# One of two shifted copies on VectorE, and tile 7's projection moved ahead of its scores, in a transformer block on one core

## What is computed

```python
h = _layernorm(x, ln1_g, ln1_b)
x = _attention(h, h, sa_wq, sa_wk, sa_wv, sa_wo, sa_bo) + x
h = _layernorm(x, ln2_g, ln2_b)
x = _attention(h, cond_emb, ca_wq, ca_wk, ca_wv, ca_wo, ca_bo) + x
h = _layernorm(x, ln3_g, ln3_b)
p = h @ ff_w1 + ff_b1
a, gate = (p[..., :D_FF], p[..., D_FF:])
h = a * jax.nn.gelu(gate, approximate=False) @ ff_w2 + ff_b2
return h + x
```

## Time and profile before

| | us |
|---|---|
| median of 3 runs | 1036.98 |
| lowest and highest | 1036.61, 1037.45 |
| profiled execution, its own time | 1036.71 |
| its span, first to last instruction | 1034.9 |
| TensorE matmul busy | 977.6 |
| VectorE busy | 822.6 |
| ScalarE busy | 621.2 |
| GpSimd busy | 401.2 |

### The profile page before, as it was taken

The page is one execution under the profiler, slowest core; times in us unless marked ns, Lnnn a source line. Parts: engine busy times, 40 slices in busy tenths (PEclk is TensorE's granted clock), DMA queues, the critical chain, the costliest instruction groups (busy, mean ns, idle before and its releaser), DMA issues.

```text
span 1034.9 us, 29709 instructions
## 1 busy us (share of the span) xinstructions
PE 977.6 (94%) x12770; PEld 739.3 (71%) x12770; DVE 822.6 (79%) x940; ACT 621.2 (60%) x1152; POOL 401.2 (39%) x380
## 2 busy tenths in 40 slices
PE   8999999999999999999999999997999999999998
PEld 6666666666666777666666666665678888888887
DVE  4788888889999877989888889998868898554433
ACT  4756656676766766676666676665754544443322
POOL 5114543444553344545534344431333345701000
PEclk9999999999999999999999999998999999999999
DMA  8695545475363644474564654564310001100000
GB/s 183 181 200 126 120 84 129 98 138 126 72 134 71 146 108 99 100 148 96 93 142 98 122 122 82 124 178 80 71 39 22 1 11 43 50 1 21 22 10 31
DMA packets 178114, 96.27 MB, mean 93 GB/s; under 512 B 141120, under 2 KB 158016, under 8 KB 177600
## 3 DMA queue, kind: packets, MB, share of 16 engines
q1 hardware_dynamic: 177984, 94.38, 41.3%
HBM read 56.60 MB, written 12.58 MB: 67 GB/s over the span
## 4 chain that ended last, share of the span: by engine, by line
PE 47%; issue 25%; POOL 16%; DVE 8%; ACT 3%; DMA 0%; POOLq 0%; DVEq 0%; SPq 0%; ACTq 0%
PE W L671 10%; PE SC L749 8%; PE SC L642 7%; POOL X L499 7%; PE W L608 4%; PE W L759 4%; POOL QKT L452 3%; PE W L927 3%; PE W L618 3%; DVE nmax L1249 3%; PE SC L737 2%; POOL QKT L449 2%; PE W L684 1%; ACT OTF L1028 1%; POOL X L487 1%
## 5 line engine op out<-in xcount | busy, mean ns | idle before, releaser
L1013 ACT ACTIVATE PR<-SC,nmax 128x1024 f32<-128x1024 f32 x256 | 286.8, 1124 | 193.9 <-DVE nmax L1249 193.6
L1249 DVE TENSOR_REDUCE nmax<-SC 128x1 f32<-128x1024 f32 x256 | 306.1, 1210 | 58.1 <-PE SC L642 55.8
L1254 DVE STREAM_TRANSPOSE PR<-PR 128x1024 f32<-128x1024 f32 x256 | 314.9, 1236 | 14.4 <-ACT PR L1013 4.4
L499 POOL TENSOR_TENSOR X<-f_raw,X 128x512 f32<-128x512 f32 x128 | 162.8, 1290 | 395.9 <-ACT f_raw L1040 395.9
L671 PE MATMUL W<-PR,V 32*64 32x256 f32 x8192 | 242.0, 380 | 4.1 <-ACT QKF L987 2.5
L642 PE MATMUL SC<-QKT 64*128 64x512 f32 x768 | 232.2, 420 | 8.7 <-ACT PR L1013 8.6
L642 PE MATMUL SC<-QKS 64*128 64x512 f32 x768 | 231.9, 419 | 7.8 <-ACT PR L1013 7.7
L671 PEld LDWEIGHTS W<-PR,V 32*64 32x64 f32 x8192 | 187.4, 132 | 53.5 <-issue 22.3
L642 PEld LDWEIGHTS SC<-QKT 64*128 64x128 f32 x768 | 127.1, 185 | 50.3 <-ACT PR L1013 21.1
L642 PEld LDWEIGHTS SC<-QKS 64*128 64x128 f32 x768 | 127.0, 185 | 49.5 <-ACT PR L1013 21.1
L1040 ACT ACTIVATE f_raw<-W,rden 128x256 f32<-128x256 f32 x256 | 102.1, 485 | 0.7 <-POOL X L499 0.3
(11 more groups left out here) (137 smaller groups left out, 1613.9 us busy)
## 6 DMA issues: line engine op xcount, KB each, us to landing
V<-scratch_v SPq DMA_DIRECT2D x128, 256.0 KB, 4.9
QKS<-QKT SPq DMA_DIRECT2D x96, 256.0 KB, 3.9
scratch_v<-VST SPq DMA_DIRECT2D x32, 256.0 KB, 4.5
wo<-in_L_xattn_sa_wo_dram SPq DMA_DIRECT2D x64, 64.0 KB, 3.8
f_raw<-in_L_xattn_ff_w_dram SPq DMA_DIRECT2D x12, 256.0 KB, 3.0
X<-in_x_dram SPq DMA_DIRECT2D x4, 512.0 KB, 5.3
w_raw<-in_L_xattn_sa_wk_dram SPq DMA_DIRECT2D x16, 128.0 KB, 4.6
w_raw<-in_L_xattn_sa_wq_dram SPq DMA_DIRECT2D x16, 128.0 KB, 3.7
```

What stands on the lines that cost most here:

```text
L499: nc.gpsimd.tensor_tensor(xs, f_raw[:, k % 2, :], xs, ALU.add).then_inc(p_x, 1)
L1013: nc.scalar.activation(PR[:, NT * s + t, :], SC[t % 2][:, :], ACT.Exp, bias=nmax[:, t % 4:t % 4 + 1], accum_out=den[:, s, t:t + 1]).then_i ...
L1249: V.tensor_reduce(nmax[:, t % 4:t % 4 + 1], SC[t % 2][:, :], AX, ALU.max, negate=True).then_inc(d_max, 1)
L1254: V.transpose(tile, tile).then_inc(d_tr, 1)
```

## The change

`gather` makes only the first of the two copies. `add_halves` on VectorE makes the other one first, signals a new semaphore `d_oc`, waits for it and for ScalarE's copy, and adds. VectorE's transpositions of tiles 4 and 5 both follow the maximum of tile 6. ScalarE scales bank 0 ahead of the exponential of tile 5, banks 1 and 2 ahead of that of tile 7, and the last one ahead of that of the next head's tile 0. On TensorE the q/k projection of tile 7 stands directly behind `project_sums`, ahead of the scores of tile 7, and waits for the first scaled bank there. All this holds for iterations that follow a head that is not plain; the last head, outside the loop, gets only the new copy.

```diff
@@ early(h)
+        def early(h):
+            return h > 0 and h - 1 not in PLAIN
@@ TensorE
-                    if h > 0 and h - 1 not in PLAIN and t == 6:
+                    if early(h) and t == 6:
                         project_sums(h - 1)
+                        for g, n, bank in PROJ_AT.get((h, 7), []):
+                            pe.wait_ge(a_op, 4 * (h - 1) + 1)
+                            project(g, n, W[:, bank, :])
...
-                    for g, n, bank in PROJ_AT.get((h, t), []):
+                    for g, n, bank in [] if t == 7 and early(h) else PROJ_AT.get((h, t), []):
...
-                        elif h > 0 and h - 1 not in PLAIN:
-                            pe.wait_ge(a_op, 4 * (h - 1) + 1)
@@ ScalarE
-                    for to, of, col in ((DH, 0, 0), (0, DH, 2 * P)):
-                        nc.scalar.copy(OTF[to:to + DH, BANK:2 * BANK].rearrange("p (a n) -> p a n", a=4),
-                                       W[of:of + DH, :, col:col + P]).then_inc(a_ot, 1)
+                    nc.scalar.copy(OTF[DH:P, BANK:2 * BANK].rearrange("p (a n) -> p a n", a=4), W[0:DH, :, 0:P]).then_inc(a_ot, 1)
...
-                    elif t == 6 and h > 0:
+                    elif t == 5 and early(h):
                         scale_out(h - 1, 0)
+                    elif t == 7 and early(h):
                         scale_out(h - 1, 1)
+                        scale_out(h - 1, 2)
...
                     elif t == 0 and h > 1:
-                        scale_out(h - 2, 2)
                         scale_out(h - 2, 3)
@@ VectorE
-                dve.wait_ge(a_ot, h + 1 + summed(h))
+                dve.wait_ge(s_pv, 8 * (h + 1))
                 dve.wait_ge(s_op, 4 * h)
+                V.tensor_copy(OTF[0:DH, BANK:2 * BANK].rearrange("p (a n) -> p a n", a=4), W[DH:P, :, 2 * P:3 * P]).then_inc(d_oc, 1)
+                dve.wait_ge(d_oc, summed(h))
+                dve.wait_ge(a_ot, h + 1)
                 V.tensor_tensor(OTF[:, 0:BANK].rearrange("p (t a i) -> p a t i", a=4, i=Q),
...
-                    if t > 0 and not (t == 3 and h > 0 or t == 5 and summing):
+                    if t > 0 and not (t == 3 and h > 0 or t in (5, 6) and summing):
                         turn(*divmod(NT * h + t - 1, NT))
                     if t == LAST_BURST and summing:
-                        turn(h, t)
                         add_halves(h - 1)
+                    if t == 6 and summing:
+                        turn(h, 4)
+                        turn(h, 5)
```

More of the change, by code:

```diff
@@ L160, in build_block @@
         s_sc = sem("s_sc"); d_max = sem("d_max"); a_exp = sem("a_exp"); d_tr = sem("d_tr"); d_rd = sem("d_rd")
-        s_pv = sem("s_pv"); a_ot = sem("a_ot"); d_ot = sem("d_ot"); s_op = sem("s_op"); a_op = sem("a_op")
+        s_pv = sem("s_pv"); a_ot = sem("a_ot"); d_oc = sem("d_oc"); d_ot = sem("d_ot"); s_op = sem("s_op"); a_op = sem("a_op")
         s_wt = sem("s_wt"); a_wt = sem("a_wt"); s_m = sem("s_m"); a_m = sem("a_m"); d_m = sem("d_m")
@@ L679, in project_out @@
                 if k == 0:
-                    pe.wait_ge(a_ot, h + 1 + summed(h))
+                    pe.wait_ge(a_ot, h + 1)
                     pe.wait_ge(m_wo[h % 2], 32 * (h // 2 + 1))
```

## The result

| | before | after |
|---|---|---|
| median of 20 runs each, us | 1037.03 | 1032.65 |
| lowest to highest | 1032.94 to 1040.22 | 1030.32 to 1036.67 |
| ratio, 95% interval | | 0.9962 (0.9950 to 0.9974) |
| profiled execution, its own time | 1036.71 | 1032.92 |
| its span | 1034.9 | 1031.1 |

The change gains 4.4 us, 0.4%. Each kernel has one profiled execution, and its own time lies up to 3.4 us off the median of that kernel.

The account below looks back on a forecast made before the run. TensorE, busy 94%, is the engine to fill, but V's eviction would hold the burst: 18 regular iterations x 0.09 = +1.6 us, the others +2.7, in all +4.3 on 1036.71, so 1041.0 us; forecast's own range 1037 to 1045, overall 1034 to 1045.5.

Parts of the forecast that it names:

- The mechanism: Regular iterations: addition 0.53 us earlier, tile 7's scores 0.95 later, then the burst waits for V's eviction and starts 0.09 later.
- The copy: VectorE's copy of one half after the gather, put at 0.66 us, bounds 0.59 to 0.75; addition 0.53 us earlier.
- G: Start of the gather's copies, from which the next burst is counted: G + 12.80 us before the change.
- The largest term: VectorE's maximum of tile 7 behind the start of its scores on TensorE, put at 1.15 us.
- The second: Length of tile 7's projection on TensorE, between output projection and tile 7's scores, put at 1.66 us.
- Two handoffs: ScalarE's scaling to TensorE's projection, put at 0.13 us, and V's eviction to the burst, put at 0.25 us.
- three terms: Bounds: copy 0.59 to 0.75 us, handoff to TensorE 0.06 for 0.13, handoff to the burst 0.20 for 0.25.
- (A): Rival: V's eviction does not hold the burst, TensorE's work does; burst 0.47 us earlier, 1031 us; chance 0.12.
- (B): Rival: VectorE's copy streams two elements at a time and takes 0.40 us; 1035 us in all; chance 0.12.
- (C): Rival: the two copies do not overlap, both reading the same four banks; addition 0.59 us later, 1055 us; chance 0.06.
- My sign of being wrong: Iterations of 21.6 us or less, where 22.1 was forecast; most likely at the step from exponential 0 to the burst.
- The irregular iterations: 9 and 26 together +1.0 us, 11 the whole 0.67, 27 +0.6, 28 and 29 0.2 each; together +2.7.

Follow-up runs that it names:

- early eviction: Kernel after, with ScalarE's eviction of tile 7's q or k projection taken from tile 1 to tile 0, ahead of exponential 0: 1025.87 us, 0.9892 of before.
- late transposition: Kernel after, with VectorE's transposition 6 behind the maximum of the next head's tile 0: 1023.14 us, 0.9878 of before; with 12 more starting matmuls 1022.56 us.
- the order alone: Kernel after, with both copies on ScalarE, the addition waiting for both, and VectorE's order of before: 1044.33 us, 1.0085 of before.
- the copy twice: Kernel after, with VectorE's copy made twice, one behind the other, 25 times: 1051.38 us, 1.0149 of before.
- the copy alone: Kernel before, with only the VectorE copy and its order of transpositions: 1035.82 us, 0.9998; the same with 12 more starting matmuls: 1035.15 us, 0.9985.

## Why the prediction was wrong

**The mechanism stood.** The copy runs beside ScalarE's, the projection fills the time up to tile 7, and the burst then waits for the V eviction. What failed is the size of small terms in the chain of fifteen from G to the burst, and the sign of their sum hung on them. The step that failed most is the one from tile 7's projection to maximum 7: the projection put at 1.66 us, measured 1.57, and the maximum put 1.15 behind its scores, measured 1.03.

| step, after | put at, us | measured | error |
|---|---|---|---|
| copy, then addition, then output projection | 1.43 | 1.47 | +0.04 |
| to the first scaling | 1.21 | 1.21 | 0.00 |
| scaling to tile 7's projection | 0.98 | 0.89 | -0.09 |
| the projection itself | 1.66 | 1.57 | -0.09 |
| first scores of tile 7 to maximum 7 | 1.15 | 1.03 | -0.12 |
| maximum 7, transposition 6, maximum 0, exponential 0 | 3.50 | 3.52 | +0.02 |
| exponential 0 to the V eviction | 2.12 | 2.06 | -0.06 |
| V eviction to the burst | 0.84 | 0.74 | -0.10 |
| G to the burst | 12.89 | 12.49 | -0.40 |

(Scaling 523.49 to projection 524.38 is 0.89, projection to scores 525.95 is 1.57, scores to maximum 526.98 is 1.03, and so on from the rows above.) 18 x 0.40 = 7.2 us would turn the forecast of 1041.0 into about 1034.

**The largest term was a misreading.** I took 527.10 to 528.25 of the earlier trace rows as the time that a maximum needs behind its scores. The last of these rows, which stands between those that I read, says otherwise, and the first two, of the same timelines, have the value that I needed:

```profile
517.18 0.49 PE L642 MATMUL SC<-QKS 64*128 64x512 f32 x1
...
518.21 2.36 DVE L1249 TENSOR_REDUCE nmax<-SC 128x1 f32<-128x1024 f32 x2 [0.79 <-PE SC L642]
...
527.08 1.25 DVE L1254 STREAM_TRANSPOSE PR<-PR 128x1024 f32<-128x1024 f32 x1
```

The last is VectorE's transposition 5 in the kernel before, and it ran until 528.33. The maximum stood behind it in the queue and not behind the scores. An interval between two engines is a latency only if nothing else held the second; here 1.15 was an upper bound and I used it as a value. At 518.21 VectorE did wait for the scores that had started at 517.18: 1.03, as in after.

**The second was of the same kind.** 528.00 to 529.66 was read as the length of a projection. ScalarE's exponential 6, for which the next scores wait, ended at 528.38 + 1.14 = 529.52, and its row sum and handoff come on top. In after, where the exponential is long done, the projection takes 1.57. In before, the next projection, which nothing holds, takes 1.60 (530.55 to 532.15).

**Two handoffs came from far rows.** 0.13 from scaling to TensorE was taken from the last head; here it is 0.05 (523.49 + 0.84 = 524.33, projection at 524.38). I had 0.06 as the other end and priced it rightly at -1.5 us. The step from eviction to burst is 0.15 (532.56 + 0.59 = 533.15, burst 533.30), not 0.25 and not the bound of 0.20.

**The copy** is 0.69, in all 25 places, like the addition, and not 0.66: the one term that I had too low. The Trainium skill, "VectorE: DVE Perf Modes", "The TRN2 errata", gives an estimate of 0.66 by its row for PSUM sources; the same section's other formula, (512 + 151) / 0.96 GHz for an fp32 addition, gives 0.69 and is what both the addition and this copy show.

**The bounds were too narrow.** I let three terms vary. The two that were misread had no bounds at all, since I took each for a measured duration. The five errors that carry weight had one sign. For the two misread ones there is a reason for it: an interval in which something else was the holder can be too long for the step, never too short. Of the other three, the two handoffs were single rows from stretches with other work around them, and the third was an overlap that I estimated: V's eviction 1.02 behind the first of q and k, where it is 0.96 (531.60 to 532.56).

**The rivals.** (A) gave 1031, nearest to the result, and its mechanism did not happen: its condition was exponential 0 to burst under 2.40 us, and that step is 2.80. The early eviction and the late transposition settle it: with the hold gone the iteration falls from 21.73 to 21.35. A forecast by A would have been near by luck. (B) is excluded by the 0.69, (C) by the common start at 520.81 and the unchanged lengths.

**My sign of being wrong did not show.** I said that I was wrong if iterations were 21.6 or less, and most likely at the step from exponential 0 to the burst. They are 21.73, and the forecast was wrong all the same; that step is 2.80 for 2.96, 0.16 of the 0.40.

**The irregular iterations.** 9 and 26 cost 0.35 each where I had 0.5, and 27 0.4 for 0.6. Iteration 28 gained. The 0.67 that I gave to iteration 11 did not come: the burst behind it waits 0.65 longer (2.16 us for 1.51), and the iteration is 0.01 longer. Iteration 12 cost 0.95, and not for VectorE's centring: after the wait of 2.16 us TensorE ran in part at half clock. In the version with the order alone and in that with the copy twice the wait is as long (2.14, 2.15), the clock stays full, and iteration 12 takes 23.14 and 23.15 us, less than the 23.23 of before and 1.0 less than in after.

**What of the gain is which part.** The copy with the transpositions put off brings 0.34 per regular iteration. The order of scalings and projection costs 0.04 there, beside the copy, and 0.21 without it. After against the two versions with the copy alone is 1032.65 against 1035.15 and 1035.82, so the order still brings 2.5 to 3 us in total. 1.1 of that is iteration 28; the remainder lies in pauses and half-clock stretches that move with each version, and I cannot assign it to the order.

## What to carry to other kernels

When a change turns on the difference of two long chains, take every step from a row in which the profile names the step's cause as the releaser. For any other interval write zero or the handoff as its lower bound, and look at what ran on the second engine just before. And when a freed wait comes back further on, look for what in that chain nobody needs yet: here one transposition, moved behind a maximum, gave twice as much again as the change (9.5 us beside 4.4).

## What the runs showed of the hardware

**After a wait of about 2 us the clock may fall or not.** Ahead of the first burst of iteration 12, TensorE waits for the eviction of q and k, and that for GpSimd. In the kernel after, in before, with the order alone, with the late transposition, and with the late transposition and 12 more matmuls at the start:

```profile
303.29 5.28 PE L675 MATMUL W<-PR,V 32*64 32x256 f32 x128 [2.16 <-ACT QKF L992]
```
```profile
305.78 3.71 PE L671 MATMUL W<-PR,V 32*64 32x256 f32 x128 [1.51 <-ACT QKF L987]
```
```profile
307.15 3.71 PE L675 MATMUL W<-PR,V 32*64 32x256 f32 x128 [2.14 <-ACT QKF L992]
```
```profile
298.82 5.40 PE L675 MATMUL W<-PR,V 32*64 32x256 f32 x128 [1.70 <-ACT QKF L992]
```
```profile
300.49 3.71 PE L675 MATMUL W<-PR,V 32*64 32x256 f32 x128 [1.70 <-ACT QKF L992]
```

The same 128 matmuls take 5.28 us after an idle time of 2.16 and 3.71 after one of 2.14; 5.40 and 3.71 after the same 1.70. Of the twelve kernels four wait 1.15 to 1.51 us here, and the clock stays full in all four. Eight wait 1.70 to 2.16, and it falls in five of them. So a wait of this length goes with the fall and does not decide it; what does, these runs do not show. The stretches around them, first after, then before (length, busy times, clock, DMA share, GB/s):

```profile
303.50:308.00 4.50, 4.50 (x120) 3.44 (x123) 4.50 (x6) 1.83 (x4) 3.77 (x5) 0.66 1.05 164
```
```profile
305.50:309.50 4.00, 3.72 (x130) 3.33 (x130) 4.00 (x6) 1.89 (x4) 3.81 (x5) 1.00 1.26 196
```

The granted clock is 0.66 on the mean of that stretch: half speed (1.2 GHz) for some 3 us of it and full speed (2.4 GHz) for the rest. Before, the attention has one such stretch, at 710.9 to 717.8; after has three, at 303, 686 and 706. They are why iteration 12 is longer in after (+0.95), as the two versions with the same wait and full clock show, and a part of why 29 is longer (+1.36) and 30 shorter (-1.26).

**Two engines read the same four PSUM banks at once** from different partitions and neither slows: 0.58 us on ScalarE, as in before, and 0.69 on VectorE, as in the second of the two copies above, which runs when ScalarE's is done.
